# A change of groups in a surface-flow kernel: one unit at a time, edge rows from their neighbours

## The reference

```python
def step(u, _):
    ux, uy, uxx, uxy, uyy = _derivs(u)          # Sobel 3x3, and Sobel of Sobel
    g2 = ux * ux + uy * uy
    ...                                          # curvatures K and H from these fields
    diff = jnp.clip(alpha * K + beta * H, -1.0, 1.0)
    u = u + DT * diff
    u = jnp.pad(u[:, :, 1:-1, 1:-1], ((0, 0), (0, 0), (1, 1), (1, 1)), mode='edge')
    return (u, None)
u, _ = jax.lax.scan(step, x, None, length=TIME_STEPS)
return 0.7 * u + 0.3 * x
```

## Time and profile before

| | us |
|---|---|
| runs: lowest, median, highest | 26116.84, 26127.3, 26135.39 |
| profiled execution | 26112.68 |
| its span on the core | 26110.8 |
| TensorE busy | 25254.3 |
| VectorE busy | 22854.9 |
| ScalarE busy | 21904.2 |
| GpSimd busy | 5859.1 |

### The profile page before, as it was taken

One profiled execution on the slowest core, in us unless ns is written; L12 is line 12 of the kernel. 1 busy time (PEld: TensorE's weight loads), 2 busy tenths in 40 slices (PEclk: granted clock), 3 DMA queues, 4 the chain that ended last, 5 costly groups with the idle time before them and its releaser, 6 DMA issues. The chain is left out here.

```text
span 26110.8 us, 751511 instructions
## 1 busy us (share of the span) xinstructions
PE 25254.3 (97%) x307482; PEld 14779.1 (57%) x307482; DVE 22854.9 (88%) x22334; ACT 21904.2 (84%) x18946; POOL 5859.1 (22%) x6804
## 2 busy tenths in 40 slices
PE   9999999999999999999999999999999999999899
PEld 5555555555646645564555467555645664664455
DVE  7777777799999999999999999999999999999222
ACT  7777777799989999998999899999989998999111
POOL 0000000133323332332333233333323332333000
PEclk9999999999999999999999999999999999999999
DMA  2111212488888888888888888888888888888655
GB/s 35 34 34 34 34 34 34 82 157 156 156 169 155 157 164 161 156 155 168 156 157 155 170 156 157 164 163 156 156 168 156 157 156 170 155 157 159 112 113 99
DMA packets 1550252, 3436.74 MB, mean 132 GB/s; under 512 B 547440, under 2 KB 679152, under 8 KB 1546480
## 3 DMA queue, kind: packets, MB, share of 16 engines
q0 software_dynamic: 805120, 2858.13, 60.5%
q1 hardware_dynamic: 742512, 536.70, 10.2%
HBM read 294.28 MB, written 201.33 MB: 19 GB/s over the span
## 5 line engine op out<-in xcount | busy, mean ns | idle before, releaser
L947 PE MATMUL surf_ps<-surf_u,surf_matf 64*64 64x512 f32 x87040 | 18772.6, 590 | 366.8 <-SPq L917 176.8
L952 PE MATMUL surf_ps<-surf_deriv,surf_matf 64*64 64x512 f32 x54400 | 12000.9, 591 | 0.0
L947 PEld LDWEIGHTS surf_ps<-surf_u,surf_matf 64*64 64x64 f32 x87040 | 7249.6, 133 | 6040.3 <-issue 4864.0
L952 PE MATMUL surf_ps<-surf_rest,surf_matf 64*64 64x512 f32 x32640 | 7234.4, 589 | 4.4 <-DVE surf_rest L1160 2.6
L952 PEld LDWEIGHTS surf_ps<-surf_deriv,surf_matf 64*64 64x64 f32 x54400 | 3842.3, 133 | 1469.3 <-issue 884.9
L1009 ACT ACTIVATE surf_deriv<-surf_ps 128x2048 f32<-128x2048 f32 (+1 forms) x2718 | 3932.7, 1447 | 844.1 <-PE surf_ps L952 841.0
L1026 ACT ACTIVATE surf_rest<-surf_deriv 128x3072 f32<-128x3072 f32 x1360 | 3756.1, 2762 | 282.9 <-DVE surf_deriv L1130 233.9
L1083 POOL DMA_DIRECT2D surf_u<-surf_ds x2720 | 2274.3, 973 | 4862.6 <-DVE surf_ds L1177 4373.3
L1160 DVE SCALAR_TENSOR_TENSOR surf_rest<-surf_deriv 128x2048 f32<-128x2048 f32 x1360 | 3108.0, 2285 | 0.0
L1156 DVE SCALAR_TENSOR_TENSOR surf_rest<-surf_rest,surf_deriv 128x2048 f32<-128x2048 f32 x1360 | 3107.6, 2285 | 0.3
L952 PEld LDWEIGHTS surf_ps<-surf_rest,surf_matf 64*64 64x64 f32 x32640 | 2305.2, 133 | 877.9 <-issue 527.9
(11 more groups left out here) (110 smaller groups left out, 31066.3 us busy)
## 6 DMA issues: line engine op xcount, KB each, us to landing
surf_rest<-surf_rest POOLq DMA_DIRECT2D x4080, 512.0 KB, 5.9
surf_u<-surf_ds POOLq DMA_DIRECT2D x2720, 258.0 KB, 5.1
att_xin<-in_x SPq DMA_DIRECT2D x2048, 41.2 KB, 2.1
attended<-att_out_rows SPq DMA_DIRECT2D x1024, 64.0 KB, 2.0
surf_u<-attended SPq DMA_DIRECT2D x512, 128.0 KB
chain_us<-flowed SPq DMA_DIRECT2D x512, 128.0 KB, 3.8
chain_xs<-attended SPq DMA_DIRECT2D x512, 128.0 KB, 4.1
out<-chain_outs SPq DMA_DIRECT2D x504, 128.0 KB, 2.8
```

The source lines that it names most:

```text
L947: mm = pe.matmul(dst[out, bank(par, phase, CROSS, t), :], matf[rows, mat, :], u[rows, k, t, off + 2:off + 2 + W], start=(i == 0), stop=(i ...
L952: mm = pe.matmul(dst[out, bank(par, phase, DIAG, t), :], matf[rows, mat, :], field(*fields[i], rows=rows, lo=t * W + off, n=W), start=(i = ...
```

## The change

`store_pair` and `load_pair` become `store_unit` and `load_unit`, with four DMAs for a middle unit. At a change of groups SP now goes through the 17 units in their order. For each it waits until that unit is updated, stores it, waits until all it has issued has landed, releases the unit before it, and issues the load of this unit. The copies of edge rows inside SBUF are gone from the change of groups: the edge row of a plane in DRAM is stored from the row beside it (row 1 for row 0) by a DMA of its own, and the block's main store leaves that row out.

```diff
--- before.py
+++ after.py
@@ -809,19 +809,36 @@
                 sp.wait_ge(moved, c)
                 sp.sem_inc(batches, 1)
 
-            def load_pair(g, j):
-                units.load_pair(sp, u, x1, g, j, moved)
-
             def load_rests(g):
                 units.load_rests(sp, u, x1, g, moved)
 
-            def store_pair(g, j):
+            def rows_of(images, img, lo, hi):
+                return images[bass.ds(img, 1), HALO + lo:HALO + hi, :].rearrange("a p w -> p (a w)")
+
+            def store_unit(g, j, i):
+                moves = 0
                 for t in range(2):
                     img = g * GI + (j + t * HI)
-                    for b in range(2 * KT):
+                    for b in (2 * i, 2 * i + 1):
                         lo, hi = OWNED[b]
-                        sp.dma_start(u10[bass.ds(img, 1), HALO + TOP[b] + lo:HALO + TOP[b] + hi, :].rearrange("a p w -> p (a w)"),
-                                     u[R * (b % 2) + lo:R * (b % 2) + hi, unit0(j) + b // 2, t, 2:W + 2]).then_inc(moved, 16)
+                        base, unit = R * (b % 2), unit0(j) + i
+                        if b == 0:
+                            sp.dma_start(rows_of(u10, img, 0, 1), u[1:2, unit, t, 2:W + 2]).then_inc(moved, 16)
+                            lo, moves = 1, moves + 1
+                        if b == 2 * KT - 1:
+                            sp.dma_start(rows_of(u10, img, TOP[b] + R - 1, TOP[b] + R), u[P - 2:P - 1, unit, t, 2:W + 2]).then_inc(moved, 16)
+                            hi, moves = R - 1, moves + 1
+                        sp.dma_start(rows_of(u10, img, TOP[b] + lo, TOP[b] + hi), u[base + lo:base + hi, unit, t, 2:W + 2]).then_inc(moved, 16)
+                        moves += 1
+                return moves
+
+            def load_unit(g, j, i):
+                for t in range(2):
+                    img = g * GI + (j + t * HI)
+                    for b in (2 * i, 2 * i + 1):
+                        sp.dma_start(u[R * (b % 2):R * (b % 2) + R, unit0(j) + i, t, 2:W + 2],
+                                     rows_of(x1, img, TOP[b], TOP[b] + R)).then_inc(moved, 16)
+                return 4
 
             def store_rests(g):
                 for t in range(2):
@@ -893,30 +910,29 @@
             def boundary(g, done, before, load):
 
                 c = before
-                for j in range(HI):
-                    if j == FIRST:
-                        sp.wait_ge(updated, done + REST_UNIT + 1)
+                order = [(j, i) for j in range(HI) for i in range(KT)]
+                order.insert(REST_UNIT, None)
+                for k, of in enumerate(order):
+                    sp.wait_ge(updated, done + k + 1)
+                    if of is None:
                         store_rests(g)
                         c = c + 16 * rests
-                        landed(c)
-                        if load:
+                    else:
+                        c = c + 16 * store_unit(g, *of)
+                    landed(c)
+                    if load:
+                        if k > 0:
+                            sp.sem_inc(unit_ready, 1)
+                        if of is None:
                             load_rests(g + 1)
                             c = c + 16 * rests
-                            landed(c)
-                            sp.sem_inc(unit_ready, 1)
-                    sp.wait_ge(updated, done + unit0(j) + KT)
-                    c = c + 16 * edge_rows(j)
+                        else:
+                            c = c + 16 * load_unit(g + 1, *of)
+                if load:
                     landed(c)
-                    store_pair(g, j)
-                    c = c + 16 * loads_pair
-                    landed(c)
-                    if load:
-                        load_pair(g + 1, j)
-                        c = c + 16 * loads_pair
-                        landed(c)
-                        sp.sem_inc(unit_ready, KT)
-
-            BD = 16 * (2 * (loads_pair * HI + rests) + 2 * HI)
+                    sp.sem_inc(unit_ready, 1)
+
+            BD = 16 * (2 * (loads_pair * HI + rests) + 4 * HI)
             GROUP_MOVES = (STEPS - 1) * EX + BD
             if GROUPS > 1:
                 with sp.Fori(0, GROUPS - 1) as g:
```

## The result

| | median us of 4 runs | lowest to highest |
|---|---|---|
| before, same chip | 26,122.9 | 26,116.8 to 26,135.4 |
| changed | 26,370.2 | 26,353.6 to 26,379.3 |

The ratio is 1.0093, 95% interval 1.0076 to 1.0111: slower by 0.9%, 247 us. The forecast was slower by 528 us, 26,655, with a range down to 26,260. The sign and the mechanism held; the size was less than half of the forecast.

The account below looks back on a forecast made before the run. At a change of groups the hot (busiest) DMA engine was taken as the bound: 26112.7 us + 481 (seven changes at 68.7) + 47 at the last = 26640.7, as a median 26,655; range 26,260 to 26,950.

Parts of the forecast that it names:

- 61 rows on one engine: Stores of end blocks: 61 is prime, so one DMA engine carries 61 packets, where two had 31 each.
- The release of pairs gives way to a wait for units and for the exchange: TensorE at changes of groups: L917's wait becomes waits for single releases and the exchange, over 50 us per change.
- the sum for one change, 68.7 us: Each change of groups with loads: 144.3 us of packets, 326.9 of GpSimd's traffic, then the exchange; TensorE loses 68.7 us.
- The packet's price: SP queue's stores and loads at a change: each packet takes 0.098 us of an engine; 1472 packets take 144.3 us.
- GpSimd's part: GpSimd's accumulating DMAs on the hot engine during one change: 28.3 slots at 11.55 us, 326.9 us.
- The check against 286.4 us: Kernel before, first change, 7191.9 to 7478.3: 72.5 us of packets plus 211.4 of GpSimd's traffic, 283.9 of 286.4 us.
- The exchange, 40 us with one slot to cover it: After SP's packets at a change: the exchange's first half takes 40 us, TensorE's work covering no more than one slot.
- The last change, +47: Stage's end, no loads: 117.6 us of packets plus 184.8 of slots, done at 24232 instead of 24185.3, +47 us.
- the lower bound: Each change: packets at the tail's 0.084 us and a hidden exchange, +22 us per change, +153; at the end nothing.
- even spread: Rival, stores at changes of groups: 61 rows spread over all engines, none hot; faster, 25,785 us; chance 0.09.
- The earlier start pays: Rival, changes of groups: SP's 41 us earlier start and smaller bursts balance the longer queue; 26,127 within 50 us; chance 0.05.
- SP's chain at the price under load: Rival, SP's queue at changes: loaded packet price, 0.34 us, holds throughout, end unit 45 us; total 27,270 us; chance 0.13.

## Why the prediction was right in sign and wrong in size

- **61 rows on one engine**: right. The packet count shows it, and cutting off one row turns 247 us of loss into 349 of gain.
- **The release of pairs gives way to a wait for units and for the exchange**: right in kind. The exchange took 5.29 us of it in the first change, not the 26 that 40 us leave beyond one slot. The waits come to 56 us there (50.9 for releases), as the prediction's sign had it. Updates across the change took 75 us more than steady (32 in 500.9 us), not over 100.
- **The step that failed: the sum for one change, 68.7 us.** The first change measured 24.1, the mean of seven 29.5. Two terms were too large.
  - *The packet's price.* I took 0.098 us, a mean over 16 engines and the small packets too. A lone engine that always has a next packet needs 0.080. With it the sum gives 1472 x 0.080 + 326.9 = 444.7 us, to 7595.3; SP ended at 7590.8. GpSimd's part was 72.9% of 440.2, 321 us instead of 326.9, as a mean over the 16 engines. So the price of the packets made some 26 of the 31 us by which SP ended sooner, GpSimd's part the rest. The check against 286.4 us did not show the error, because two errors nearly cancel in it: the packets were 740 x 0.080 = 59 us and not 72.5, GpSimd's part 77.6% of 286.4 = 222 and not 211.4. That 283.9 came so close was luck in part. What 0.080 does not explain is the 0.11 us that a further packet costs above 31 per end block; that difference stays open.
  - *The exchange, 40 us with one slot to cover it.* Before, its issues took 7532.1 to 7571.6, with GpSimd's traffic beside them; just behind a wait of TensorE they took 7590.8 to 7614.1. TensorE also stood one unit earlier than I had it: the release of unit 15 waits for the store of unit 16, so both come at the end, at 7582.9 and 7590.8, and 21 us of the exchange lay beside TensorE's work. From SP's last landing to TensorE's start it was 26.4 us (7590.8 to 7617.2) instead of 40. This term was 14 us per change.
  - Together: SP's part ended 31 us earlier than forecast (7590.8 for 7621.8), the exchange took 14 us less, and TensorE started the step 45 us earlier (7617.2 for 7661.8). 68.7 less 45 is what the first change measured.
- **The last change, +47**: too large for the same reason. From the update of unit 0 to the chain's first issue it is 280.2 us (24138.6 to 24418.8), before 255.5 (23929.8 to 24185.3): 25 more. With 1200 packets at 0.080 the forecast's sum gives 280.8 for 302.4.
- **Bounds**: the lower bound, 0.084 and a hidden exchange, gave 22 us per change. It lay nearer than the value I took, and I gave that side too little weight.
- **Rivals**: even spread was priced at 25,785 and measures 25,774 once the rows allow it, so the price was right and the condition was not met. "The earlier start pays", 26,127 within 50 us, is refuted by the result itself, 26,370. SP's chain at the price under load did not come: its end unit of 45 us measured 33 to 37, and once 14.

## What to carry to other kernels

Look at how a transfer's rows divide before looking at its bytes: one row less made 62 rows 61, took the store from two engines to one and doubled the queue on the busiest. Here the cure alone, 62 rows stored as 60 + 2 in the kernel before, gained 270 us. Find it by counting small packets in the DMA view and by a low flat tail in GB/s; cure it by cutting the rows so that nearly all go on 14 to 16 engines. And when a sum rests on one busy resource, price it where that resource works alone, and go through who stands where at the moment when the wait ends.

## What the runs showed that I had not expected

A share of 102% of all DMA engines, evenly spread, costs TensorE under 2% of its matmuls in that stretch (920 for 936), while end units with 130 packets on one engine, a share of 5.1% for SP in the first of them, stop it twice for some 25 us in the first change. In the changed kernel the waits for VectorE's H term fell from 138.4 to 68.3 us although the hot engine got half as many packets again: perhaps because GpSimd's traffic came in a thinner stream with the waits for releases. That last is an inference; no run was made for it.
